# Quantised weights unpacked with outputs on partitions and turned by TensorE, and eight bias additions moved into the steps of a later stage

## The reference

```python
def quant_ffn(x):                                    # qweight (512, 384) int32, 3 words -> 4 weights
    p = qweight.reshape(512, 128, 3)
    v = stack([p[:, :, 0] & 63, p[:, :, 0] >> 6 & 63, p[:, :, 1] & 63, p[:, :, 2] & 63], axis=2)
    w = (v.reshape(512, 512) - weight_zero_point) * weight_scale     # both (512, 1): one per output
    return einsum('bsk,nk->bsn', x, w) + bias
x = L0_attn_u                                        # (1, 2048, 512) float32
x = x + 0.5 * quant_ffn(layernorm(x))
x = x + s4_convolution(layernorm(x), layer 0)        # kernel of 512 taps from a Cauchy sum, and D * u
x = x + 0.5 * quant_ffn(layernorm(x))
x = x + 0.5 * (silu(xn @ W_gate.T) * (xn @ W_up.T)) @ W_down.T       # xn = layernorm(x), F = 1376
x = x + s4_convolution(layernorm(x), layer 1)
x = x + 0.5 * (the same gated FFN)(layernorm(x))
```

## Time and profile before

| | us |
|---|---|
| median of the three runs | 899.4 |
| the profiled execution's own time | 899.31 |
| its span in the profile | 897.5 |
| TensorE busy in it | 879.1 (98%) |
| DVE busy | 620.2 (69%) |
| POOL busy | 366.1 (41%) |
| ScalarE busy | 314.2 (35%) |

### The profile page before, as it was taken

The page is one execution under the profiler, slowest core; times in us unless marked ns, Lnnn a source line. Parts: engine busy times, 40 slices in busy tenths (PEclk is TensorE's granted clock), DMA queues, the critical chain, the costliest instruction groups (busy, mean ns, idle before and its releaser), DMA issues.

```text
span 897.5 us, 11743 instructions
## 1 busy us (share of the span) xinstructions
PE 879.1 (98%) x4116; PEld 721.1 (80%) x4116; DVE 620.2 (69%) x1058; ACT 314.2 (35%) x517; POOL 366.1 (41%) x728
## 2 busy tenths in 40 slices
PE   8999999999999999999999999999999999999998
PEld 4778887778888877888888878888888788888876
DVE  7989787799989786655565876555667865454553
ACT  4534457444444351322223532222233511122211
POOL 6858668723323343332334452323344532222211
PEclk8999999999999999999999999999999999999999
DMA  9200000066677775565655665464646667556455
GB/s 333 97 1 1 1 1 2 29 252 263 253 281 265 244 232 176 165 187 145 183 152 164 193 171 183 136 188 128 194 146 212 190 177 243 171 184 209 129 156 172
DMA packets 41358, 148.27 MB, mean 165 GB/s; under 512 B 3538, under 2 KB 3794, under 8 KB 39892
## 3 DMA queue, kind: packets, MB, share of 16 engines
q0 software_dynamic: 29040, 100.93, 37.4%
q1 hardware_dynamic: 12260, 46.59, 13.7%
HBM read 117.36 MB, written 30.15 MB: 164 GB/s over the span
## 4 chain that ended last, share of the span: by engine, by line
PE 81%; DVE 6%; POOL 5%; DMA 3%; issue 3%; ACT 1%; SPq 0%; POOLq 0%; DVEq 0%; ACTq 0%
PE front L1457 15%; PE front L1459 15%; PE front L1458 15%; PE acc L1411 8%; PE acc L1413 7%; PE acc L1412 7%; DMA down_weights<-saved_down 3%; PE front L476 3%; PE acc L1340 2%; PE acc L1339 2%; PE acc L1338 2%; POOL x_rows L788 1%; POOL rstd L458 1%; DVE hidden_lo L1241 1%; PE front L1340 1%
## 5 line engine op out<-in xcount | busy, mean ns | idle before, releaser
L1457 PE MATMUL front<-row_operands_hi,weight_operands 128*128 128x512 f32 x616 | 241.7, 392 | 2.0 <-DVE snapshots L1201 1.8
L1459 PE MATMUL front<-row_operands_hi,weight_operands 128*128 128x512 f32 x616 | 239.9, 389 | 0.0
L1458 PE MATMUL front<-row_operands_lo,weight_operands 128*128 128x512 f32 x616 | 239.8, 389 | 0.0
L1201 DVE TENSOR_TENSOR snapshots<-front,snapshots 128x512 f32<-128x512 f32 x132 | 91.0, 689 | 78.8 <-PE front L1459 77.3
L1411 PE MATMUL acc<-down_weights,hidden_hi 128*128 128x512 f32 x352 | 140.0, 398 | 5.3 <-DMA down_weights<-saved_down 3.7
L1457 PEld LDWEIGHTS front<-row_operands_hi,weight_operands 128*128 128x128 f32 x616 | 115.7, 188 | 27.3 <-DVE weight_operands L611 2.2
L1413 PE MATMUL acc<-down_weights,hidden_lo 128*128 128x512 f32 x352 | 137.3, 390 | 0.0
L1412 PE MATMUL acc<-down_weights,hidden_hi 128*128 128x512 f32 x352 | 137.2, 390 | 0.0
L1459 PEld LDWEIGHTS front<-row_operands_hi,weight_operands 128*128 128x128 f32 x616 | 115.6, 188 | 24.2
L1458 PEld LDWEIGHTS front<-row_operands_lo,weight_operands 128*128 128x128 f32 x616 | 115.7, 188 | 23.4
L827 POOL DMA_DIRECT2D weight_operands<-saved_weights x66 | 48.6, 736 | 188.5 <-PE front L1459 173.3
(11 more groups left out here) (177 smaller groups left out, 1342.7 us busy)
## 6 DMA issues: line engine op xcount, KB each, us to landing
weight_operands<-saved_weights POOLq DMA_DIRECT2D x33, 1280.0 KB, 6.4
down_weights<-saved_down POOLq DMA_DIRECT2D x77, 512.0 KB, 4.0
saved_weights<-weight_operands SPq DMA_DIRECT2D x11, 1792.0 KB, 8.0
weight_operands<-saved_weights POOLq DMA_DIRECT2D x33, 512.0 KB, 4.4
raw_weights<-wgu SPq DMA_DIRECT2D x11, 512.0 KB, 3.8
saved_down<-down_weights SPq DMA_DIRECT2D x11, 512.0 KB, 3.3
x_rows<-x_in SPq DMA_DIRECT2D x3, 1024.0 KB, 11.5
raw_down<-wdown SPq DMA_DIRECT2D x11, 256.0 KB, 2.9
```

Of the source, the lines that this page charges most:

```text
L1201: V.tensor_tensor(out, sum_of(k, product)[:], other, ALU.add).then_inc(front_read, 1)
L1457: T.matmul(o, wh, xh, start=(j == 0), stop=False)
L1458: T.matmul(o, wh, xl, start=False, stop=False)
L1459: last = T.matmul(o, wl, xh, start=False, stop=(j == 1))
```

## The change

**Weights.** The host passes the words as they are, with outputs on partitions: 384 words a partition and block, and zero point and scale as one column each of `params`. DVE unpacks a block with three `tensor_scalar` on strided views (value 0, value 1, and values 2 and 3 of each group of four) into `q_unpacked`, and a fourth subtracts the zero point and multiplies by half the scale, both a value per partition (POOL makes `half_scale`). TensorE transposes the 16 blocks of 128 x 128 into `acc[0]` to `acc[3]` (`transpose_weights`). ScalarE rounds from there once all are in, and DVE makes all four low parts; POOL makes none. Two of the three spreading products are gone, the bias's goes into `front[3]`. Zeros are multiplied 12, 2 and 3 times, into `front[2]`. The DMAs of shifts, zero points and scales are gone; the bias row is loaded behind the weights, tiles 0 to 3 one by one.

**Order.** The first eight sums use four banks; the Cauchy products wait for update 7. Items 3 to 6 are transposed behind products 1 to 3. On DVE the statistics of items 4 to 6 come before xt_lo(3), those of item 7 after update 0. On ScalarE xt_hi(3) comes after normalisation 5.

**Biases.** Those of the third stage's items for tiles 8 to 15 are not added two items ahead any more, but after the update, by POOL, one in each of the first eight steps of the first unit.

```diff
+            if l < EARLY:
+                return acc[(0, 1, 3, 2)[l % BLK]]
+            return acc[(0, 1, 3)[(l - EARLY) % 3]] if l < TILES else acc[(l + 1) % (BLK - 1)]
+
+
+        EARLY = 2 * BLK
+
+        def bias_is_last(n):
+
+
+            return ITEMS[n].kind == "quant" and (n < TILES or ITEMS[n].tile >= UTILES)
...
             load_first_x(0)
-            sp.dma_start(rows[:, 0:2, :], qrows.unsqueeze(0)).then_inc(rows_in, 16)
-            sp.dma_start(rows[:, 2, :], qbias.unsqueeze(0)).then_inc(rows_in, 16)
-            sp.dma_start(qsh[:], qshift).then_inc(shift_in, 16)
+            load_quantised(0)
             sp.dma_start(ident[:], table_in[:, IDENT:IDENT + P]).then_inc(ident_in, 16)
-            load_quantised(0)
             load_first_x(1)
-            for j in range(1, KT):
-                load_quantised(j)
+            for i in range(1, KT):
+                load_quantised(i)
+            sp.dma_start(rows[:], qbias.unsqueeze(0)).then_inc(rows_in, 16)
+            load_first_x(2)
+            load_first_x(3)
...
-                if n >= BIAS_LAG and bias_is_last(n - BIAS_LAG):
+                if BIAS_LAG <= n < TILES + BIAS_LAG:
                     bias_step(n - BIAS_LAG)
-                if TILES <= n + BIAS_AHEAD < PRE and ITEMS[n + BIAS_AHEAD].kind == "quant":
+                if n + BIAS_AHEAD < PRE and ITEMS[n + BIAS_AHEAD].kind == "quant" and not bias_is_last(n + BIAS_AHEAD):
...
+                    if k < UTILES:
+                        bias_step(last_biases[k])
+                    if k == UTILES:
+                        pool.wait_ge(bias_added, 2 * TILES)
...
+                act.wait_ge(q_transposed, 1)
+                nc.scalar.activation(Qh[:, j, :], acc[j][:], ACT.Copy).then_inc(dequant_hi, 1)
...
             norm_step(act, 1)
-            for j in range(2):
+            xt_hi_step(act, 0)
+            act.wait_ge(bias_spread, 1)
+            nc.scalar.activation(biasB[:], front[3][:], ACT.Copy).then_inc(bias_ready, 1)
+            xt_hi_step(act, 1)
+            norm_step(act, 2)
+            for j in range(KT):
                 dequant_round(j)
-                xt_hi_step(act, j)
-                norm_step(act, j + 2)
-            act.wait_ge(rows_spread, 3)
-            nc.scalar.activation(biasB[:], acc[1][:], ACT.Copy).then_inc(bias_ready, 1)
-            dequant_round(2)
-            dequant_round(3)
             xt_hi_step(act, 2)
-            xt_hi_step(act, 3)
+            norm_step(act, 3)
             norm_step(act, XT_SLOTS)
             den_scale()
             for n in range(XT_SLOTS + 1, NORM_AHEAD):
                 norm_step(act, n)
+            xt_hi_step(act, 3)
...
-            def dequantise(j):
-                dve.wait_ge(quant_in[j], 16)
-                link(V.tensor_scalar(qraw[:, j, :], qraw[:, j, :], qsh[:, 0:1], 63,
-                                     ALU.logical_shift_right, ALU.bitwise_and))
-                link(V.tensor_tensor(wq[:, j, :], qraw[:, j, :], acc[2][:], ALU.subtract))
-                V.tensor_tensor(wq[:, j, :], wq[:, j, :], acc[3][:], ALU.mult).then_inc(dequant_ready, 1)
+            def dequantise(i):
+
+                dve.wait_ge(quant_in[i], 16)
+                whole = lambda t: t[:, i].rearrange("p g c -> p (g c)")
+                for into, word, shift in (((0, 1), (0, 1), 0), ((1, 2), (0, 1), 6), ((2, 4), (1, 3), 0)):
+                    V.tensor_scalar(quant[:, i, :, slice(*into)], qraw[:, i, :, slice(*word)], shift, 63,
+                                    ALU.logical_shift_right, ALU.bitwise_and).then_inc(unpacked, 1)
+                dve.wait_ge(unpacked, 3 * (i + 1))
+                V.tensor_scalar(wq[:, i, :], whole(quant), par[:, ZERO_POINT + i:ZERO_POINT + i + 1],
+                                half_scale[:, i:i + 1], ALU.subtract, ALU.mult).then_inc(dequant_ready, 1)
+
+            def dequant_lo(j):
+                dve.wait_ge(dequant_hi, j + 1)
+                V.tensor_tensor(Ql[:, j, :], acc[j][:], Qh[:, j, :].bitcast(F32), ALU.subtract).then_inc(dequant_split, 1)
...
             early_stats(0)
+            dve.wait_ge(half_scale_ready, 1)
+            dequantise(0)
             early_stats(1)
-            dve.wait_ge(shift_in, 16)
-            dve.wait_ge(rows_spread, 2)
-            dequantise(0)
-            early_stats(2)
-            early_stats(3)
             dequantise(1)
             dequantise(2)
+            early_stats(2)
+            dequantise(3)
             xt_lo_step(dve, 0)
-            dequantise(3)
             xt_lo_step(dve, 1)
-            for j in range(HALF, KT):
-                dve.wait_ge(dequant_hi, j + 1)
-                V.tensor_tensor(Ql[:, j, :], wq[:, j, :], Qh[:, j, :].bitcast(F32), ALU.subtract
-                                ).then_inc(dequant_split_last, 1)
-            early_stats(4)
+            for j in range(KT):
+                dequant_lo(j)
+            early_stats(3)
             xt_lo_step(dve, 2)
+            for n in range(XT_SLOTS, STATS_AHEAD - 1):
+                early_stats(n)
             xt_lo_step(dve, 3)
-            for n in range(XT_SLOTS + 1, STATS_AHEAD):
-                early_stats(n)
+            update_step(dve, 0)
+            early_stats(STATS_AHEAD - 1)
...
-                if ITEMS[n].kind == "quant" and not bias_is_last(ITEMS[n].number):
+                if ITEMS[n].kind == "quant" and not bias_is_last(n):
                     dve.wait_ge(bias_added, quant_number(n) + 1)
-                if is_light(n):
+                if n and is_light(n):
                     update_step(dve, n)
...
+                    T.matmul(front[2][:], zeros[:, 0:P], zeros[:, P:P + D], start=True, stop=True)
             pe.wait_ge(zeros_made, 1)
-            multiply_zeros(9)
-            pe.wait_ge(rows_in, 32)
-            pe.wait_ge(spread_ready, 2)
-            T.matmul(acc[2][:], spread[:, ONES, :], rows[:, 0, :], start=True, stop=True).then_inc(rows_spread, 1)
-            T.matmul(acc[3][:], spread[:, HALVES, :], rows[:, 1, :], start=True, stop=True).then_inc(rows_spread, 1)
+            multiply_zeros(12)
+
+            def transpose_weights(i):
+
+                pe.wait_ge(dequant_ready, i + 1)
+                for j in range(KT):
+                    last = T.transpose(acc[j][:, i * P:(i + 1) * P], wq[:, i, j * P:(j + 1) * P], ident[:])
+                if i == KT - 1:
+                    last.then_inc(q_transposed, 1)
+
             pe.wait_ge(ident_in, 16)
+            transpose_weights(0)
             transpose_step(pe, 0)
+            pe.wait_ge(rows_in, 16)
+            pe.wait_ge(spread_ready, 1)
+            T.matmul(front[3][:], spread[:], rows[:], start=True, stop=True).then_inc(bias_spread, 1)
+            transpose_weights(1)
             transpose_step(pe, 1)
-            T.matmul(acc[1][:], spread[:, HALVES, :], rows[:, 2, :], start=True, stop=True).then_inc(rows_spread, 1)
-            multiply_zeros(9)
+            multiply_zeros(2)
+            transpose_weights(2)
+            multiply_zeros(3)
+            transpose_weights(3)
             transpose_step(pe, 2)
-            transpose_step(pe, 3)
-            multiply_zeros(4)
...
+                pe.wait_ge(light_updated, EARLY)
                 pe.wait_ge(inv_den_ready, 2 * KT)
...
-                    elif l >= 3:
+                    elif BLK <= l < EARLY + 3:
+                        pe.wait_ge(light_updated, l - 3)
+                    elif l >= EARLY + 3:
                         pe.wait_ge(light_updated, l - 2)
...
                 if n == 1:
-                    transpose_step(pe, XT_AHEAD)
-                if n and n + XT_AHEAD < PRE:
+                    pe.wait_ge(bias_ready, 1)
+                    transpose_step(pe, 3)
+                if n == 2:
+                    transpose_step(pe, 4)
+                    transpose_step(pe, 5)
+                if n == 3:
+                    transpose_step(pe, 6)
+                if n >= 3 and n + XT_AHEAD < PRE:
                     transpose_step(pe, n + XT_AHEAD)
```

89 lines of the change are left out of this document (39 added, 50 removed).

## The result

| | before | changed |
|---|---|---|
| median of 14 runs | 900.58 us | 903.83 us |
| lowest and highest | 898.18, 903.83 | 901.98, 905.87 |
| profiled execution's own time | 899.31 | 903.34 |
| span | 897.5 | 901.5 |
| TensorE granted clock, mean over the span | 0.996 | 0.992 |

The ratio is 1.0029, with a 95% interval of 1.0019 to 1.004: the change makes the kernel slower, by 2.6 us by the ratio, 3.3 by the medians, 4.0 in the profiled executions. The forecast was 897.8 us with a range of 895.0 to 902.5, and the changed kernel's median lies above both.

The account below looks back on a forecast made before the run. The prediction took DVE up to `den_i`, then POOL, to bound the first 48 us, TensorE afterwards. Start -0.2, third stage -2.3 and unit 0 +1.0 sum to -1.5 on 899.31: 897.8 us, range 895.0 to 902.5.

Parts of the forecast that it names:

- What bounds the start: First 48 us: DVE up to den_i, then POOL, set the clock; Cauchy products at 48.1, -0.2 us.
- The DVE sum: Start, DVE: four weight blocks at 1.4 us each plus statistics, fourth block ready at 11.7, first product near 13.7.
- The step that failed first: Start: TensorE transposes the fourth weight block at once (12.2), ScalarE rounds from 12.4, after tile 2's normalisation.
- rival (a): Start: TensorE at 1.2 GHz delays the weights, transposes end at 15.3, Cauchy at 51.1, total 900.7 us; chance 0.28.
- POOL's part: Start: POOL loses two low parts, gains a 4-wide product in front of all rstd; claimed to cost nothing.
- xt_lo(3): Start, DVE: stands still from 19.2 to 22.1 at this operation, waiting for ScalarE's xt_hi(3).
- The step that failed worst: Start: TensorE's 3 us lead is given back in waits at item 8's transposes and at Cauchy, without cost.
- Third stage: Eight biases leave POOL's queue at items 42 to 53, so TensorE's waits for normalised tiles shrink: -2.3 us.
- Unit 0: First unit: one POOL bias a step, behind DVE's copy, delays the hidden product: +1.0 us over eight steps.
- Rival (b): First unit: POOL's bias passes DVE's waiting copy, costing +7 us instead of +0.7 over seven steps, 904 us; chance 0.10.
- (c): Start: DVE's 2.9 us gap before xt_lo(3) doesn't come, den_i and Cauchy 2.9 earlier, total 895.6 us; chance 0.13.
- (d): Third stage: moved biases give nothing because DVE's statistics hold the transposes anyway, +0.8, total 900.1 us; chance 0.07.

Follow-up runs that it names:

- e7_zeros_at_start: The changed kernel with ten more products of zeros in TensorE's waits between 5 and 11 us: 904.35 us, ratio 1.0037 to the kernel before.
- e5_pool_order: The changed kernel with POOL's rstd of item 2 ahead of the Cauchy numerators instead of behind them: 905.65 us, ratio 1.005 to the kernel before.
- e13_transposes_earlier: The changed kernel with start zeros, rstd, statistics and xt_hi(3) reordered, and transposes of items 3 to 6 each one product earlier: 899.23 us, ratio 0.9971.
- e12_late_with_zeros: The kernel before with four more POOL operations ahead of its last invert, and nine products of zeros in TensorE's wait before Cauchy: 904.31 us, ratio 1.0031.
- e10_reordered_zeros: The changed kernel with its start reordered, zeros in TensorE's first waits, and four products of zeros ahead of the Cauchy products: 902.15 us, ratio 1.001.
- e3_zeros_both_waits: The changed kernel with seven products of zeros ahead of item 8's transposes and six ahead of the Cauchy products: 903.7 us, ratio 1.0035.

## Why the prediction was wrong

**What bounds the start** was right: DVE up to `den_i`, then POOL. `den_i` to Cauchy is 19.33 us before and 19.32 after, and "an earlier first product is worth nothing unless it moves 48.28" is what happened. From xt_lo(3) to `den_i` the sum had 6.6 us, and 6.61 were measured.

**The DVE sum.** Four blocks at 1.4 us and the fourth ready near 11.7: measured 12.06, with blocks of 1.1 to 1.2, but the statistics of tile 1 waited 1.04 us for their tile. By the rule of the Trainium skill ("VectorE: DVE Perf Modes", Mode 2×_2P) that one tensor is read through both ports, the prediction had a block near 1.2, and the trace agrees better with that than with the 1.4 that was taken.

**The step that failed first** is "TensorE transposes the fourth block at once (12.2), ScalarE rounds from 12.4, after tile 2's normalisation". TensorE did it at 14.46, at 1.2 GHz, and normalisation 2 was at 14.02. The first is rival (a), which had 15.3 for the end of these transposes (measured 15.1) and 51.1 for Cauchy (50.96). It got 0.28 where it should have led: it said itself that the same stretch was at 1.2 GHz before. That its 51.1 fits so well is in part luck, since without this lock the other would have held the rounding to 14.46 (`e7_zeros_at_start`), only 0.65 us earlier. The second was nowhere in the text. POOL's part was closed with "nothing, since tile 0's rstd waits for tile 0"; nobody asked what stands ahead of rstd of item 2.

**xt_lo(3)** was right in kind and size: a stand of 2.9 us foreseen, 3.02 measured, only shifted by the late weights.

**The step that failed worst** is "TensorE, 3 us early at its first product, gives it back in two waits". Both waits were found, and priced at nothing because they end at the same moment either way. They cost 3.1 us more, since TensorE's clock fell behind the second; behind the first it fell too, and that only shortened the second wait (1.13 us, and 2.73 in `e5_pool_order`, where it stayed up). The forecast used the granted clock only for the first 15 us, where a row showed it at 0.50, and did not ask what a new wait does to it elsewhere. Rival (a) had the same hole, so its 900.7 was 2.6 short of the profiled 903.34.

**Third stage**: -2.3 forecast, -2.39 measured. **Unit 0**: +1.0 forecast, +0.98 measured. The mechanism was right: the copy first, then the bias, then the hidden product, 1.07 us long on record where 1.2 to 1.3 was forecast. The Trainium skill's statement ("SBUF — State Buffer", Who interferes with whom) that whichever issued first holds the port for its whole length agrees with the trace in both places: 1.29 us from the copy's end at 214.33 give 215.62 for the bias's end (215.50), and 0.69 from there 216.2 for the hidden product's (216.04). Rival (b) did not happen. But the 0.98 is that of a profile in which the clock did not fall in unit 0, and that was luck: in nine of the thirteen profiles with moved biases it did (last section).

**Rivals (c) and (d)** did not happen. By its own terms (c) comes to 895.8 us, not 895.6. What it described, DVE's gap of 3 us gone, was later made by hand, in `e13_transposes_earlier`. It took zeros at the start and another order of `rstd`, statistics, xt_hi(3) and transposes, and the Cauchy products came 2.3 us before those of the kernel before; (c) had them 3.1 before.

## What to carry to other kernels

A wait of TensorE that "only gives back a lead" is not free: behind it the engine can run at half speed for several us, here 1.6 or some 3 us of loss for waits from 0.66 us up. When a change lets TensorE arrive early at a place that something else releases, either shorten the chain that releases it, or put products of zeros into the whole wait; zeros in a part of it gave 1.1 us (`e12_late_with_zeros`) or nothing (`e10_reordered_zeros`), and zeros in an earlier wait as well opened the later one again (`e3_zeros_both_waits`).

When one lock is found, ask at once what would hold the same work without it. Here each of two edits alone gave nothing at the Cauchy products, and both gave 1.75 us there.
